# Three PSUM banks for the score units of the maxima, one bank for a half's products and their transposes

## The reference

```
scores = jnp.einsum('bhqd,bhkd->bhqk', q, k) / np.sqrt(HEAD_DIM).astype(np.float32)
scores = jnp.where(causal, scores, -jnp.inf)
attn = jax.nn.softmax(scores, axis=-1)
out = jnp.einsum('bhqk,bhkd->bhqd', attn, v)
...
x = x + 0.5 * _L0_ffn_ref(_layernorm(x, axis=-1), L0_ffn_w1, L0_ffn_b1, L0_ffn_w2, L0_ffn_b2)
x = x + _L0_attn_ref(_layernorm(x, axis=-1), L0_attn_Wq, L0_attn_Wk, L0_attn_Wv, L0_attn_Wo)
x = x + 0.5 * _L0_ffn_ref(_layernorm(x, axis=-1), L0_ffn_w1, L0_ffn_b1, L0_ffn_w2, L0_ffn_b2)
```

## Time and profile before

| what | us |
|---|---|
| median of three runs | 651.38 |
| lowest, highest | 648.69, 651.41 |
| the profiled execution, its own time | 651.7 |
| its span | 649.7 |
| PE busy in the span | 601.7 (93%) |
| DVE busy | 454.9 (70%) |
| ACT busy | 334.5 (51%) |
| POOL busy | 253.0 (39%) |

### The profile page before, as it was taken

One profiled execution on the slowest core, in us unless ns is written; L12 is line 12 of the kernel. 1 busy time (PEld: TensorE's weight loads), 2 busy tenths in 40 slices (PEclk: granted clock), 3 DMA queues, 4 the chain that ended last, 5 costly groups with the idle time before them and its releaser, 6 DMA issues. The chain is left out here.

```text
span 649.7 us, 17478 instructions
## 1 busy us (share of the span) xinstructions
PE 601.7 (93%) x6340; PEld 503.8 (78%) x6340; DVE 454.9 (70%) x914; ACT 334.5 (51%) x589; POOL 253.0 (39%) x447
## 2 busy tenths in 40 slices
PE   1899999998679999999999999999998799999997
PEld 1688888887457787887878788788675588888886
DVE  5967777776477776776767767677663377777764
ACT  2434444443215666655666557665656344444442
POOL 5843334441545443344433434333212233333330
PEclk9979999999889999999999999999999899999999
DMA  8420000000585665456554565555610000000001
GB/s 277 143 66 1 0 0 0 0 1 6 157 236 148 171 176 166 129 150 192 151 152 136 147 195 148 149 144 151 195 53 3 1 32 32 32 32 32 32 32 33
DMA packets 71139, 63.41 MB, mean 98 GB/s; under 512 B 4130, under 2 KB 64322, under 8 KB 71106
## 3 DMA queue, kind: packets, MB, share of 16 engines
q1 hardware_dynamic: 69922, 62.81, 33.4%
q10 hardware_dynamic: 1184, 0.14, 0.2%
HBM read 33.03 MB, written 29.36 MB: 96 GB/s over the span
## 5 line engine op out<-in xcount | busy, mean ns | idle before, releaser
L650 DVE TENSOR_REDUCE mx<-bank 128x2 f32<-128x512 f32 (+1 forms) x192 | 124.1, 688 | 39.7 <-PE bank L820 39.6
L399 PE MATMUL bank<-w2q,g_hi 128*128 128x256 f32 x512 | 125.7, 286 | 3.1 <-DVE g_lo L299 2.8
L356 ACT ACTIVATE g<-bank,b1c 128x512 f32<-128x512 f32 x128 | 88.3, 690 | 70.3 <-PE bank L394 66.9
L399 PE MATMUL bank<-w2q,g_lo 128*128 128x256 f32 x512 | 123.8, 283 | 0.0
L749 ACT ACTIVATE probs<-bank 128x512 f32<-128x512 f32 x192 | 111.9, 597 | 16.6 <-PE bank L820 9.2
L399 PEld LDWEIGHTS bank<-w2q,g_hi 128*128 128x128 f32 x512 | 97.7, 191 | 4.8 <-DVE w2q L306 1.9
L399 PEld LDWEIGHTS bank<-w2q,g_lo 128*128 128x128 f32 x512 | 97.8, 191 | 0.7
L299 DVE TENSOR_TENSOR g_lo<-g,g_hi 128x512 fp32r<-128x512 f32 x128 | 86.1, 704 | 3.5
L394 PE MATMUL bank<-xt_hi,w1q 128*128 128x512 f32 x256 | 81.7, 401 | 1.5 <-PEq L504 1.5
L394 PE MATMUL bank<-xt_lo,w1q 128*128 128x512 f32 x256 | 81.4, 399 | 0.0
L820 PE MATMUL bank<-k,q 99*64 99x128 bf16 (+1 forms) x1024 | 74.7, 246 | 0.0
(11 more groups left out here) (98 smaller groups left out, 1018.4 us busy)
## 6 DMA issues: line engine op xcount, KB each, us to landing
qk_slots<-parts SPq DMA_DIRECT2D x32, 384.0 KB, 3.5
q<-qk_slots SPq DMA_DIRECT2D x32, 384.0 KB, 4.0
k<-qk_slots SPq DMA_DIRECT2D x32, 384.0 KB, 4.8
qk_slots<-parts SPq DMA_DIRECT2D x32, 256.0 KB, 3.0
res<-x SPq DMA_DIRECT2D x8, 512.0 KB, 3.6
qk_slots<-parts SPq DMA_DIRECT2D x32, 128.0 KB, 3.2
out<-res SPq DMA_DIRECT2D x8, 512.0 KB, 2.9
w1f<-w1t SPq DMA_DIRECT2D x2, 512.0 KB, 6.5
```

The source lines that it names most:

```text
L356: nc.scalar.activation(g[:, f, :], h_bank[f % 4][:], ACT.Gelu, bias=b1c[:, f:f + 1]).then_inc(g_ready, 1)
L399: last = nc.tensor.matmul(y_bank[t % 2][:, 0:D], part[:, f, t * P:(t + 1) * P], w2q[:, f, :], start=f == 0 and part is g_hi, stop=f == FC ...
L650: nc.vector.tensor_reduce(o, i, AX.X, ALU.max).then_inc(s_done, 1)
```

## The change

The eight banks are dealt out anew. The S units turn in three banks (0, 1, 2), the T units move to banks 3 and 4 and still have two, and `PV` and `OT` share bank 5. `MT` writes into the last bank of the S ring.

```diff
-    s_ring, t_ring, o_bank, turn_bank, mixed = banks[0:2], banks[2:4], banks[4], banks[5], banks[6:8]
-    mt_bank = s_ring[1]
+    s_ring, t_ring, o_bank, mixed = banks[0:3], banks[3:5], banks[5], banks[6:8]
+    turn_bank = o_bank
+    mt_bank = s_ring[2]
...
-                    r = s_ring[n % 2][:]
+                    r = s_ring[n % 3][:]
...
-                if p.has(0) or n >= 2:
-                    pe.wait_ge(s_done, UNITS * b + n - 1)
-                if n % 6 == 1 and (p.has(0) or n > 1):
+                if p.has(0) or n >= 3:
+                    pe.wait_ge(s_done, UNITS * b + n - 2)
+                if n % 6 == 2 and (p.has(0) or n > 2):
                     pe.wait_ge(mt_sb, 2 * b + n // 6)
-                r, q, k = s_ring[n % 2], q6[par], k6[par]
+                r, q, k = s_ring[n % 3], q6[par], k6[par]
...
                 if p.has(-1) or h:
-                    pe.wait_ge(o_copied, 2 * p.p + h)
+                    pe.wait_ge(normed, 2 * p.p + h)
...
                 pe.wait_ge(o_copied, j + 1)
-                if p.has(-2) or (p.has(-1) and h):
-                    pe.wait_ge(normed, j)
```

## The result

| kernel | median of runs, us | lowest, highest | ratio to before |
|---|---|---|---|
| before | 651.39 (4 runs) | 648.69, 651.56 | |
| changed | 641.83 (4 runs) | 640.85, 642.40 | 0.9862, 95% interval 0.9837 to 0.9886 |

The change makes the kernel 9.6 us faster, 1.4%. The prediction was 642.0, range 638.5 to 646.8. The profiled execution took 640.85 us, its span is 638.9 against 649.7 before, 10.8 us less.

A forecast was written before the change was run, and what follows sets the result against it. PE was taken as the bound, with S waiting for DVE's maxima. 6.8 + 0.95 + 0.38 + 2.0 - 0.7 = 9.4 us off 651.7 gives 642.3; the median 0.3 lower, 642.0, range 638.5 to 646.8.

The forecast's parts named there:

- The loop term: In the loop's 10 periods, each of 20 half-steps saves 0.34 us, 6.8 us in all.
- the price: PV's new wait for the normalised heads costs 0.7 us once, in period 15, h = 0, and nothing in the loop.
- the fill: Period -1 and period 0, h = 0: shorter waits of S give 1.3 and about 0.7 us, 2.0 taken.
- ACT's rival: In the loop, ACT's own pace of 0.645 us per exponential becomes the limit: about 644.5 us; chance 0.14.
- The walk: One loop half-step followed unit by unit from undisturbed distances: transposes at 331.34 instead of 331.69, 0.34 us taken as saved.
- ACT's hold on T: In a loop half-step, T2 and T5 wait for exponentials and come 0.05 us late.
- DVE's pace: In a loop half-step, DVE runs six maxima without a gap in 3.88 us, and would still take 3.88.
- the full half-steps: Outside the loop, period 0, h = 1, and periods 11 and 12: five half-steps gain 0.19 us each, 0.95 together.
- the two put at nothing: Periods 13 and 14, h = 0: no gain, since MT waits there for POOL and the maxima set the end.
- The clock's rival: In the fill, PE no longer falls to the lower clock, saving up to 3.4 us more: 638.6 us; chance 0.10.
- the bounds: Fill gain is 0 if next-batch loads or the copy of `mt` are late, 3.4 us if the copy comes sooner.
- The slower rival: In loop half-steps h = 1, PV waits for the shared bank in all 15: about 655 us; chance 0.04.

The follow-up runs named there:

- e8: The changed kernel run again without any further edit; 641.33 us, ratio 0.9843.
- e10: The changed kernel run once more without further edit, in a later round; 641.62 us, ratio 0.9870.
- e3: The kernel before, with two S banks, but each maximum taken over half of the keys; 639.57 us, ratio 0.9843.
- e4: The changed kernel, with three S banks, but each maximum taken over half of the keys; 639.16 us, ratio 0.9834.
- e1: The kernel before with PV and OT sharing one bank as in the change, S keeping two banks; 650.77 us, ratio 1.0019.
- e5: The kernel before with PV and OT sharing one bank and the third bank given to T instead of S; 650.24 us, ratio 1.0.
- e6: The changed kernel, but each exponential covers 256 of the 512 columns; 636.17 us, ratio 0.9772.

## Why the prediction was right, and where it was not

**The median.** 642.0 was said and 641.83 measured. The mechanism was right in the loop, where most of the gain lies; at the two ends of the pipeline it was right in part. The close agreement is partly luck. The loop term was too large by 0.6 us, the price too small by 0.5, the fill too small by 0.5 or more. In the stages that the change touches the first pair of traces differs by 8.6 us, and the e8 and e10 traces differ from the one before by 9.2 and 9.4, where the sum said 9.4. The times have their own scatter: beside the kernel before in the later rounds, the changed kernel was 9.2 us (e8) and 8.1 us (e10) faster. And the execution of 651.7 us, from which the prediction took its 9.4 off, held a low stretch of 1.56 us at its end that isn't always there.

**What bounds it.** Right. PE is the bound, and S waited for the maxima. e3 and e4 show it from both sides, e1 and e5 show that nothing else of the edit gains in the loop. ACT's rival fell: in the changed kernel six exponentials take 3.65 us, one each 0.61, and in e5 3.05, one each 0.49. So 0.645 was waiting for T, and not ACT's own pace.

**The walk.** It gave 3.75 us from S0 to the transposes (331.34 - 327.60 is 3.74), measured were 3.78. The saving is 0.31 a half-step, not 0.34, and the loop 6.16 us, not 6.8. ACT's hold on T was sized well: the walk has 0.05 at T2 and 0.04 at T5, and e6 shows 0.08 for both. What was too short is PE's own pace. Without the two holds the walk comes to 3.65 us, and e6 takes 3.70. The undisturbed distances were read from rows rounded to 0.01 us and summed over eight distances, and a unit that had to wait also starts the next one about 0.02 later (S2 to T2 is 0.30 in the earlier trace rows), which the walk left out. One reading was off besides: S5 starts 0.08 us after the maxima of two units before (330.88), not 0.03 to 0.06.

**DVE's pace.** A reading was wrong, with little harm to the sum. I took the 3.88 us for six maxima, with no gap shown, as DVE's own pace, and said that it would stay. It fell to 3.68. The row merges instructions with gaps too small to be named. (3.88 - 0.69) / 5 is 0.638 and (3.68 - 0.69) / 5 is 0.598. By this reckoning DVE in its turn waited some 0.04 us for each S with two banks, which PE could begin only after the maxima of two units before. S and maxima were in a ring with each other, and neither was simply the slower one. e1 and e5, with two S banks and whole maxima, have the 20.4 us period. e6, with shorter exponentials, has 19.60, and all others have 19.78.

The harm is in periods 13 and 14, h = 0. The prediction put nothing there, since the maxima would not end earlier. They do. In period 13, before and changed:

```profile
460.76 3.88 DVE L650 TENSOR_REDUCE mx<-bank 128x4 f32<-128x512 f32 x6 [1.32 <-PE bank L820]
```

```profile
451.18 3.78 DVE L651 TENSOR_REDUCE mx<-bank 128x4 f32<-128x512 f32 x6 [1.32 <-PE bank L821]
```

The half-step falls by the same 0.10 us, from 7.35 to 7.25.

**Outside the loop.** For periods 11 to 14 the sum of terms was 1.14 us (four times 0.19 and 0.38), measured 1.01. That is near because two errors met: the full half-steps gained 0.13 or 0.14 each instead of 0.19, and the two put at nothing gained 0.10 each.

For the fill 2.0 was taken for the three half-steps, measured 2.54 in period -1 and period 0, h = 0, in the first trace, and 3.08 and 3.28 in e8 and e10. The ground was right only in part: the term named waits alone. The waits of S in period -1 are near what was said (0.72 us in h = 1, said 0.64), but one low stretch of the clock is missing as well, worth 1.1 to 1.3 us. The clock's rival, which had a chance of 0.10, was therefore partly true, as far as these traces tell. Of its two stretches one stayed.

In period 0, h = 0, hardly anything was gained (0.02 in the first trace, 0.18 in e8), where I had said 0.7. In e8 S2 stands 1.13 us for the copy of `mt`, where S1 stood 1.25 before. The copy, named among the bounds, comes no sooner: it starts 2.00 us after S0 in e8 (193.40) and 1.56 before (198.62 and 197.06), behind two copies and two casts of ACT, one of which waits 0.66 us for DVE.

```profile
195.40 0.36 ACT L784 COPY mt<-bank 24x256 bf16<-24x256 bf16 x1
```

In the first trace S2 does not stand. There S0 stood instead, for the loads of the next batch, the other bound, and the low stretch fell into this half-step. As the wait is ahead of S0, it is counted in period -1, which is longer than in the other traces of this kernel for it (14.85 against 14.27 and 14.47):

```profile
193.90 0.11 PEld L816 LDWEIGHTS bank<-mask_qk,ident_b 128*64 128x64 bf16 x2 [1.89 <-DMA k<-qk_slots]
```

**The price.** Period 15 costs 0.79 instead of 0.71: PV starts 0.15 us after the write of `att` ends (487.24 to 487.39), and not the 0.06 taken from the S units. The place that the prediction missed is period 0, h = 1, with 0.43 us in e1, of which 0.30 are left in the first trace. So the price is 1.2 us and not 0.7. This half-step has no ANT and no WO, because no batch is finished yet. So it lacks the cover that I had counted for "h = 1" from a row of the loop. The slower rival named the right mechanism and the wrong place: it looked at the loop, where the 1.44 us of cover were not even reduced, since DVE's work ahead of `att` hangs on ACT and so on PE.

**Not in the sum.** 0.64 us ahead of the first S unit and 1.56 us at the end. Neither is of the change.

## What to carry to other kernels

When two engines hand buffers back and forth, compare the waits of both rings before giving one of them a buffer: in the loop the third bank was worth 6.2 us in the S ring and nothing in the T ring, and where only T units are left it was worth 1.3 us in the T ring. Where a buffer is paid for by sharing another, the price stands where the pipeline fills and drains, because the work that covers the new wait is missing there; look at each half-step at the ends, not only at one of the loop. And a merged row without a named gap does not prove that the engine never waited: divide its length by the count and compare it with the duration of one.

## What was not expected of the hardware

- Instructions of DVE that follow at once start about 0.60 us apart though each takes 0.68 to 0.69 (six maxima in 3.68 us, changed kernel). The exponentials of ACT, 0.597 us each, start 0.49 apart when T is ahead (six in 3.05 us, period 15 of e5). With two T banks they start 0.585 apart there (3.52 us), because PE in turn waits for them. So the duration of one instruction is not the pace of an engine, and the pace in one stage need not be its own.
- The fill, with waits of 0.2 to 1.5 us at the S units, was granted 0.83 of the clock over 21 us before the change. The loop, with waits of 0.2 to 0.35 us in each half-step, was granted 1.00. With shorter waits in the fill it was 0.92, one low stretch of 1.7 us less. A low stretch fell at different places in traces of the same kernel.
